# A fused RWKV block with routed experts: two VectorE intermediates move from SBUF to PSUM banks

## The reference

```python
x = _ln(x, ln0_w, ln0_b)
h = _ln(x, ln1_w, ln1_b)                      # xk, xv, xr: h mixed with h of the token before
k, v = xk @ Wk.T, xv @ Wv.T
sr = sigmoid(xr @ Wr.T)
att = _wkv(w, time_first, k, v)               # a recurrence over the tokens: numerator / denominator
x = x + (sr * att) @ Wo.T
h2 = _ln(x, ln2_w, ln2_b)                     # xk2, xr2 likewise mixed
kv = square(relu(xk2 @ Wfk.T)) @ Wfv.T
x = x + sigmoid(xr2 @ Wfr.T) * kv
```

## Time and profile before

| what | value |
|---|---|
| median of 3 runs | 444.21 us (443.97 to 528.0) |
| the profiled execution, its own time | 445.68 us |
| its span in the profile | 443.9 us |
| granted clock, mean | 0.971 |

### The profile page before, as it was taken

How to read it: one execution, slowest core, us unless ns; L and a number is a source line. 1 busy time by engine, 2 the same in 40 slices (tenths; PEclk the granted TensorE clock), 3 DMA queues, 4 the chain that set the end, 5 groups by cost and what they waited for, 6 DMA issues and landing times.

```text
span 443.9 us, 9951 instructions
## 1 busy us (share of the span) xinstructions
PE 390.8 (88%) x2521; PEld 304.8 (69%) x2521; DVE 311.3 (70%) x1084; ACT 300.2 (68%) x730; POOL 253.9 (57%) x319
## 2 busy tenths in 40 slices
PE   0377888998989997999989999999999999999990
PEld 0134446766666665567535699999999999999840
DVE  6669898999997999767485566665666565665171
ACT  2577699999977785676432377777777777776064
POOL 5855757375557877787867244444444444444182
PEclk9998799999998999999999999999999999999996
DMA  7999000000000210101265267776777667761583
GB/s 221 208 347 322 5 1 0 1 1 1 0 2 31 97 39 7 46 31 51 77 216 150 89 243 248 260 254 244 250 258 256 239 246 254 258 234 69 182 309 95
DMA packets 47247, 64.86 MB, mean 146 GB/s; under 512 B 8796, under 2 KB 31068, under 8 KB 47192
## 3 DMA queue, kind: packets, MB, share of 16 engines
q1 hardware_dynamic: 42584, 54.50, 36.3%
q0 software_dynamic: 4448, 9.38, 6.2%
q10 hardware_dynamic: 160, 0.35, 0.4%
HBM read 21.65 MB, written 13.91 MB: 80 GB/s over the span
## 4 chain that ended last, share of the span: by engine, by line
PE 64%; DVE 16%; ACT 7%; issue 5%; POOL 4%; SPq 1%; DMA 1%; ACTq 0%; DVEq 0%; POOLq 0%
PE bank L1351 23%; PE bank L1369 11%; PE bank L1035 4%; PE bank L1017 4%; PE bank L1083 2%; PE bank L968 2%; PE bank L1072 2%; PE bank L1066 2%; DVE rec L569 2%; PE bank L969 2%; ACT z L718 2%; DVE bst L493 2%; POOL frs L858 2%; PE bank L1343 2%; PE bank L1401 2%
## 5 line engine op out<-in xcount | busy, mean ns | idle before, releaser
L1210 POOL DMA_INDIRECT routed_rows<-yo,goes_to x75 | 72.0, 960 | 93.9 <-DVE yo L1259 91.8
L1351 PE MATMUL bank<-xT,w 128*128 128x128 f32 x896 | 112.7, 275 | 0.0
L1351 PEld LDWEIGHTS bank<-xT,w 128*128 128x128 f32 x896 | 106.3, 192 | 0.8 <-issue 0.5
L1251 DVE SCALAR_TENSOR_TENSOR actT<-bank,tile_bias,gl 128x128 f32<-128x128 f32 x225 | 65.4, 345 | 26.9 <-PE bank L1351 23.2
L1303 ACT ACTIVATE gl<-bank,tile_bias 128x128 f32<-128x128 f32 x225 | 66.3, 364 | 15.1 <-PE bank L1351 14.9
L419 POOL DMA_INDIRECT dispatched_rows<-rows_all,slot_i x64 | 64.0, 999 | 19.2 <-issue 17.0
L1369 PE MATMUL bank<-we_sb,actT 128*128 x450 | 62.7, 275 | 0.9 <-DVE yo L1259 0.9
L1369 PEld LDWEIGHTS bank<-we_sb,actT 128*128 128x128 f32 x450 | 56.1, 192 | 1.2 <-issue 1.1
L1259 DVE SCALAR_TENSOR_TENSOR yo<-bank,goes,wb 128x128 f32<-128x128 f32 x75 | 26.3, 351 | 34.6 <-PE bank L1369 30.5
L1017 PE MATMUL bank<-xk,wfk_sb 128*128 128x512 f32 x64 | 33.8, 639 | 5.2 <-DVE xk L586 4.1
L1297 ACT ACTIVATE xT<-bank 128x128 f32<-128x128 f32 x74 | 20.5, 278 | 24.4 <-PE bank L1343 24.2
(11 more groups left out here) (215 smaller groups left out, 795.0 us busy)
## 6 DMA issues: line engine op xcount, KB each, us to landing
w<-we_sb SPq DMA_DIRECT2D x75, 384.0 KB
x_all<-dispatched_rows SPq DMA_DIRECT2D x75, 68.0 KB, 2.0
we_sb<-we SPq DMA_DIRECT2D x1, 4608.0 KB
we_sb<-routed_rows SPq DMA_DIRECT2D x8, 512.0 KB, 7.2
rows_all<-x SPq DMA_DIRECT2D x8, 256.0 KB, 5.3
out<-x_all SPq DMA_DIRECT2D x8, 256.0 KB, 2.3
routed_rows<-yo,goes_to POOLq DMA_INDIRECT x75
dispatched_rows<-rows_all,slot_i POOLq DMA_INDIRECT x64, 2.3
```

The source lines that it names most:

```text
L1210: ng.indirect_dma_start(routed, bass.IndirectOffsetOnAxis(ap=goes_to[n // U % DB][:, n % U:n % U + 1], axis=0), yo[n % YO][:, :], None).th ...
L1251: nv.scalar_tensor_tensor(actT[n % UA][:, at], ps_a[j][:, 0:P], tile_bias[:, j, n:n + 1], gl[n % 2][:, at], ALU.add, ALU.mult).then_inc(s2 ...
L1351: return nt.matmul(to[:, 0:P], w1[m][:, off:off + P], xT[m][:, :], start=True, stop=True)
```

## The change

`output(c)` writes the gated numerator into the bank po in place of yT and reads it from there; `x3(c)` writes the gated channel values into the bank pkv, in place, and reads them from there; x2c is gone. The first instruction of `output(c)` now waits until ScalarE has read po of the step before (x1_ready) and not only until TensorE has written it. The next product into pkv, and the first gate of the shared expert that uses pkv, wait for x3_ready, the second instruction of `x3`, and not for x2_step, the first.

```diff
@@ -217,7 +217,6 @@
         th2 = tmp("th2", [P, W])
-        x2c = tmp("x2c", [P, W])
         s13 = tmp("s13", [P, CT, C])
@@ -572,11 +571,11 @@
                 v.wait_ge(s["den_ready"], c + 1)
                 v.wait_ge(s["th_ready"], c + 1)
-                after(v, "po_ready", c)
-                nv.scalar_tensor_tensor(yT[:, :], th[:, :], 1.0, nd[:, 0, :], ALU.add, ALU.mult).then_inc(s["y_half"], 1)
+                after(v, "x1_ready", c)
+                nv.scalar_tensor_tensor(po[:, :], th[:, :], 1.0, nd[:, 0, :], ALU.add, ALU.mult).then_inc(s["y_half"], 1)
                 v.wait_ge(s["y_half"], c + 1)
                 v.wait_ge(s["rec_ready"], c + 1)
-                nv.scalar_tensor_tensor(yT[:, :], yT[:, :], 0.5, rec[:, :], ALU.mult, ALU.mult).then_inc(s["yT_ready"], 1)
+                nv.scalar_tensor_tensor(yT[:, :], po[:, :], 0.5, rec[:, :], ALU.mult, ALU.mult).then_inc(s["yT_ready"], 1)
@@ -591,11 +590,11 @@
                 after(v, "x3_ready", c)
-                nv.scalar_tensor_tensor(x2c[:, :], th2[:, :], 1.0, pkv[:, :], ALU.add, ALU.mult).then_inc(s["x2_step"], 1)
+                nv.scalar_tensor_tensor(pkv[:, :], th2[:, :], 1.0, pkv[:, :], ALU.add, ALU.mult).then_inc(s["x2_step"], 1)
                 v.wait_ge(s["x2_step"], c + 1)
                 v.wait_ge(s["s13_ready"], c + 1)
                 after(v, "xn_ready", c)
-                nv.scalar_tensor_tensor(x3c[:, :, :].rearrange("p n c -> p (n c)"), x2c[:, :], 0.5,
+                nv.scalar_tensor_tensor(x3c[:, :, :].rearrange("p n c -> p (n c)"), pkv[:, :], 0.5,
                                         s13[:, :, :].rearrange("p n c -> p (n c)"),
                                         ALU.mult, ALU.add).then_inc(s["x3_ready"], 1)
@@ -1029,7 +1028,7 @@
             def mixed_channels(c):
                 t.wait_ge(s["sq_act"], (c + 1) * HF)
-                after(t, "x2_step", c)
+                after(t, "x3_ready", c)
@@ -1068,7 +1067,7 @@
             def shared_gate(c, j):
                 t.wait_ge(s["expert_w_loaded"], 5 * 16)
-                bank_read(c, j, "sh_gelu", (s["ev_ready"], CH), (s["x2_step"], CH))
+                bank_read(c, j, "sh_gelu", (s["ev_ready"], CH), (s["x3_ready"], CH))
```

## The result

Over 16 runs of each kernel on the same chip the changed kernel has a median of 441.33 us and the kernel before 444.01: ratio 0.9936, with a 95% interval of 0.9921 to 0.9951, so 2.8 us saved (0.0064 x 444.01). One execution of either kernel was disturbed (1413 and 528 us) and does not enter the ratio. The profiled execution of the changed kernel took 442.21 us with a span of 440.5, 3.4 less than the span before. Lines behind L220 have moved up by one: L575 and L578 are the two steps of `output`, L593 and L597 those of `x3`, L585 is the mix.

What follows compares the result with a forecast made beforehand. No engine is full in the attention stage, the first 252 us; each waits in turn. Savings 0.95 + 0.55 + 0.57 + 0.6 = 2.7 us, less 0.3, leave 2.4: 444.2 - 2.4 = 441.8 us, range 438.9 to 445.9.

Steps and rivals of the forecast that it cites:

- Both second steps become instructions of L594's kind, 682 ns: L579 and L598, reading PSUM, take L594's median; over eight steps 1.1 and 3.1 us, together 4.2 us of VectorE time.
- The four places on the chain, 2.7 us: Stretched L579 at 58.98 and L598 at 112.18, 152.37 and 172.33 us, saving 0.95, 0.55, 0.57 and 0.6.
- The other five L598 save under 0.25 each: L598 runs outside the counted chain places, and seven L579: under 0.25 us each, hidden beside TensorE's work.
- The mix takes over part of the stall: Mix behind L598 meets GpSimd: of 0.71 us saved at 112.18, 0.55 is left; of 1.40 at 152.37, 0.57.
- PSUM writes cost 0: Sixteen VectorE writes into PSUM, by L576 and L594, priced at 0; bounds 0.06 us gained to 0.68 more each.
- D: Rival, chance 0.14: L576 and L594 writing PSUM cost up to 0.68 us each, 1.4 us slower in all, 445.6 us.
- The Trainium skill's rule: Fixed 58 cycles with SBUF source, 120 with PSUM; L579 and L598 would pay some 65 ns more each, 1.0 us total.
- The changed waits cost 0: Later waits of L576, the product into pkv and the shared gate have 11.5, 8.3 and 1.3 us of cover; no stall.
- B, the saving is absorbed: Rival, attention stage: shifted instructions catch new stalls of 0.6 to 1 us; 444.2 us, chance 0.22 shared with E.
- C, the clock: Rival, chance 0.14: with TensorE's 2.10 us wait 0.6 shorter, its clock may stay 2.4 GHz; 1.7 us more saved, 440.1.
- E: Rival: L579 and L598 stand still with a PSUM input too; time 444.2 us, chance 0.22 shared with B.
- The loop begins 2 to 3 us earlier: Sign for the forecast: the experts' loop takes the same 160 us but starts 2 to 3 us earlier.

Runs made afterwards that it cites:

- the changed kernel's other profile: The changed kernel run again unaltered, in another set on another chip, against the kernel before: 441.13 us against 443.24, ratio 0.9947.
- the time mix alone: Kernel before with only output's gated numerator in po and its wait, x3 as before; run twice, ratios 0.9975 and 0.9955 to the kernel before.
- the channel mix alone: Kernel before with only x3's gated values in pkv and its two later waits; run twice, ratios 0.9945 and 0.9937 to the kernel before.

## Why the prediction was right

The forecast was 441.8 us, 2.4 saved; measured were 441.33 and 2.8 saved. The mechanism, two-input instructions that stand still beside GpSimd, is the one that the runs show. That the size came out this near is in part luck: the sum was made from the stalls of one execution, and errors in two of its terms offset each other. By its own steps:

- **Both second steps become instructions of L594's kind, 682 ns.** Right: 692, and never more. VectorE's saving on these two lines is 8.5 + 6.5 less 16 x 0.692, that is 3.9 us for the 4.2 forecast.
- **The four places on the chain, 2.7 us.** Near in sum, 2.9, wrong in how it spreads. From the start of the first step to the end of what follows, the profiled pair gives: at 58 us 1.57 for 0.95 (3.30 from 57.32 to 60.62, now 1.73), at 111 us 0.66 for 0.55, at 150 us 0.05 for 0.57, and at 170 us 0.58 for 0.6. Of the 1.57, L579 gives the 0.95 that was forecast; the other 0.62 is L575's own stall, shorter in this profile (1.01 for 1.62) but back at 1.64 in the changed kernel's other profile: luck. TensorE's wait for this yT bears the 0.95 out: where no dip of the clock lies between 50 and 60 us, it is 1.51 or 1.52 us in the three other profiles with yT's first step in SBUF, and 0.58 and 0.59 in the time mix alone and in the changed kernel's other profile. The third place is the mis-sized one. I had GpSimd's additions stay where they were on the clock; they came 0.6 us later beside VectorE's own work (149.58 to VectorE's 149.23, where it was 151.39 to 151.65), and the mix met more of the second. The stall of 2.09 us was itself peculiar to the execution that I read: the other three profiles with both intermediates in SBUF have L598 there at 0.84 to 0.86 us, and the changed kernel's have the mix at 1.68 and 1.06. By these the change gains nothing at this place.
- **"The other five L598 save under 0.25 each."** True of their own rows, but I left out what they did to GpSimd. Near 91 and 132 us an undisturbed L598 held up GpSimd's addition, and the mix behind it; there the mix fell from 1.29 and 1.30 us to 0.82 and 0.83, and TensorE's wait for it at 133 us from 0.92 to 0.46, alike in the profiles of the channel mix alone and in the changed kernel's second. What this is worth in the whole is open: that wait stands on the chain of neither profile.
- **The mix takes over part of the stall.** The mechanism was right, the place half: whole at 150 us, nearly nothing at 111.
- **PSUM writes cost 0.** Off by a small size: 46 ns directly behind a reciprocal, about 10 elsewhere, 0.4 us in VectorE's time. I had reasoned from the reads, and with an ill-matched row: L594 does the same arithmetic as L576 (median 632 ns), not as L579 and L598. That reads are free holds all the same: the L594 that follows a reciprocal, at 111.52 us, took 628, as L576 does there. D's price of 0.68 each was never near.
- **The Trainium skill's rule**, the fixed 120 cycles with a PSUM source ("VectorE: DVE Perf Modes", on the TRN2 errata): L578 and L597 with a PSUM source have a median of 692 ns, and the same instructions without one have 692 too where GpSimd leaves them alone (L580 and L599 above). No penalty for this shape and type, in either kernel; the measurement decides.
- **The changed waits cost 0.** Held: 0.9978 and 0.9992. The release of pkv stayed covered: L597 of the last step ends at 205.20 and the gate in pkv starts at 206.53, 1.3 us later as before.
- **B, the saving is absorbed**: not for the whole, but it is what happened at 150 us. **C, the clock**: the four matmuls behind the wait at 173 took 1.98 us for 3.68, the sign that I had named, but it does not carry the theory. Of six profiles with the wait of 2.10 us, four show 1.98 and only two 3.68, so the wait of 2.10 does not by itself bring the dip; that all five with 1.53 show 1.98 fits C and does not prove it. Over the runs the mean clock is equal, so the clock adds scatter and no gain. **D** and **E** fell with the rows of the single lines.
- **The loop begins 2 to 3 us earlier**: the first product of the loop starts at 248.20 and not 251.66, 3.5 earlier in this pair, a little more than forecast; part of it is the clock (mean 0.977 for 0.971).

## What to carry to other kernels

Look at the spread of a VectorE instruction before its mean: one shape with a floor of 0.69 us and cases of 1.4 to 2.1 is held up by something, and the GpSimd timeline at the same instants named it here. Look at GpSimd's spread too (1.28 and 1.74 us): the instruction to move may be one that is never long itself. Compare more than one profile before a stall enters a sum. An intermediate that only VectorE passes to itself can go into a PSUM bank that is idle anyway; price it as the stalls that stand on the chain, less those that the next two-input instruction takes over. Check who else waits for the bank: the same trick with a bank that TensorE needs soon made the kernel 1.4 us slower, though the stall was gone.

## What the runs showed of the hardware

- VectorE's instruction with two SBUF inputs and a wide GpSimd operation stand in each other's way, in both directions: a 128x512 instruction of 0.69 us took up to 2.09 beside GpSimd's additions, and an addition of 1.28 us took 1.74 beside it. With one input in PSUM the two second steps took 0.69 in every profile, and with x3's in PSUM the addition took at most 1.30.
- A 128x512 fp32 instruction of this kind that writes PSUM takes 46 ns more than one that writes SBUF (medians 674 and 628 ns) directly behind a reciprocal, whether its inputs are both in SBUF or one is in the same bank (675 and 633). Elsewhere the write in place costs little (medians of the line 690 to 693 against 681 to 686). That reads and writes of one bank take turns, as I had bounded it, is excluded.
- The kernel's time differs by 1.4 to 2.5 us between its runs at a granted clock of 0.982 and more and those at 0.977 and less. The dips move: the kernel before had one at 175 to 180 us in one profile (0.66) and at 50 to 60 in another (0.68 and 0.64). A difference of two single profiles of this kernel is therefore uncertain by as much.
